# Reordering VectorE's token step in the front of a fused tokenizer, attention and FP4 feed-forward kernel, with one subtraction moved from GpSimd

## The reference

```python
# tokenizer
y = layernorm(patches, ln1_g, ln1_b) @ Wp + bp
h = concatenate([layernorm(y, ln2_g, ln2_b), txt], axis=1)
# differential attention, 8 heads, each the difference of two softmax maps
q, k, v = x @ Wq.T, x @ Wk.T, x @ Wv.T            # x = layernorm(h)
q, k = rotary(rmsnorm(q)), rotary(rmsnorm(k))     # 16 heads of 16
attn = softmax(q1 k1) - lam * softmax(q2 k2)      # causal
h = h + (layernorm(attn @ v) * (1 - LAMBDA_INIT)) @ Wproj.T
# feed-forward, weights and activations rounded to FP4 in blocks of 16
scale = max(|block|) / 6;  fp4(x) = grid[searchsorted(mid, |x / scale|)] * sign(x) * scale
h = h + fp4(silu(fp4(x) @ fp4(w_gate).T) * (fp4(x) @ fp4(w_up).T)) @ fp4(w_down).T
```

## Time and profile before

| what | value |
|---|---|
| median of 3 runs | 659.81 us (658.97 to 660.0) |
| the profiled execution's own time | 662.52 us |
| its span in the trace | 660.8 us |
| mean granted TensorE clock | 0.948 |
| busy share PE / DVE / ACT / POOL | 87% / 84% / 49% / 47% |

### The profile page before, as it was taken

The page is one execution under the profiler, slowest core; times in us unless marked ns, Lnnn a source line. Parts: engine busy times, 40 slices in busy tenths (PEclk is TensorE's granted clock), DMA queues, the critical chain, the costliest instruction groups (busy, mean ns, idle before and its releaser), DMA issues. The chain is left out here.

```text
span 660.8 us, 14226 instructions
## 1 busy us (share of the span) xinstructions
PE 576.4 (87%) x3666; PEld 470.0 (71%) x3666; DVE 554.1 (84%) x1444; ACT 322.1 (49%) x760; POOL 309.8 (47%) x455
## 2 busy tenths in 40 slices
PE   5665568999999999999999998589999999999996
PEld 4554455767776776777677676478888888888885
DVE  5999847898889889888988985498888888888884
ACT  2242215655665665566565564244544444445442
POOL 2455523555455445545554553155455445545542
PEclk9878776999999999999999997789999999999999
DMA  6900000011111111111111101111111111111111
GB/s 173 325 17 23 24 16 18 27 38 41 30 40 35 35 35 38 40 34 37 35 41 29 42 23 46 30 39 49 48 54 52 54 48 54 49 48 48 57 32 35
DMA packets 33734, 31.99 MB, mean 48 GB/s; under 512 B 6098, under 2 KB 32050, under 8 KB 33714
## 3 DMA queue, kind: packets, MB, share of 16 engines
q1 hardware_dynamic: 33714, 31.75, 16.3%
HBM read 23.02 MB, written 8.71 MB: 48 GB/s over the span
## 5 line engine op out<-in xcount | busy, mean ns | idle before, releaser
L741 PE MATMUL bank<-v_sb,pt 113*113 113x33 f32 x1024 | 109.1, 262 | 0.0
L741 PEld LDWEIGHTS bank<-v_sb,pt 113*113 113x113 f32 x1024 | 108.4, 181 | 0.7 <-issue 0.7
L858 POOL TENSOR_SCALAR_AFFINE_SELECT pt<-pt 113x452 f32<-113x452 f32 x128 | 73.9, 600 | 68.5 <-ACT pt L798 68.5
L798 ACT ACTIVATE pt<-bank 113x452 f32<-113x452 f32 x128 | 63.1, 545 | 38.2 <-PE bank L729 38.2
L138 PE MATMUL bank<-wgu_hi,fx_hi 128*128 128x512 f32 x174 | 69.5, 399 | 8.0 <-DVE fx_lo L1131 8.0
L1177 POOL TENSOR_TENSOR h_deq<-fh,fhb 128x704 f32<-128x704 f32 x29 | 40.3, 1389 | 68.8 <-DVE fhb L1084 56.3
L729 PE MATMUL bank<-q_blk,k_t 64*113 64x452 f32 x256 | 67.7, 605 | 0.0
L138 PE MATMUL bank<-wgu_hi,fx_lo 128*128 128x512 f32 x174 | 66.8, 384 | 0.0
L138 PE MATMUL bank<-wgu_lo,fx_hi 128*128 128x512 f32 x174 | 66.7, 384 | 0.0
L138 PE MATMUL bank<-wqkv_hi,xo_hi 128*113 128x256 f32 (+1 forms) x128 | 50.3, 393 | 17.7 <-DVE xo_lo L923 17.7
L1191 POOL TENSOR_TENSOR fh<-fh,fhb 128x704 f32<-128x704 f32 x29 | 40.3, 1391 | 42.2 <-DVE fhb L1145 42.2
(11 more groups left out here) (160 smaller groups left out, 1531.3 us busy)
## 6 DMA issues: line engine op xcount, KB each, us to landing
xb<-h_dram SPq DMA_DIRECT2D x29, 129.0 KB, 2.1
rb<-h_dram SPq DMA_DIRECT2D x29, 128.0 KB, 2.0
h_dram<-h SPq DMA_DIRECT2D x32, 112.9 KB
out<-res SPq DMA_DIRECT2D x28, 128.0 KB, 1.7
px<-in_patches SPq DMA_DIRECT2D x9, 384.0 KB, 10.1
hx<-in_txt SPq DMA_DIRECT2D x32, 77.0 KB
hr<-in_txt SPq DMA_DIRECT2D x32, 77.0 KB
wf<-in_wgu SPq DMA_DIRECT2D x1, 1408.0 KB, 8.0
```

The source lines that it names most:

```text
L741: mm = pe.matmul(pv_ps[s % 2][0:T, s // 2, :], pt[0:T, s, :], v_sb[0:T, s // 2, :], start=True, stop=True, skip_group_check=True)
L798: act.activation(pt[0:T, GS * g:GS * (g + 1), :].rearrange("p s t -> p (s t)"), sc_ps[g % 2][0:T, :], ACT.Exp, scale=1.0 / math.sqrt(HD)). ...
L858: pool.affine_select(out=grp, in_=grp, compare_op=ALU.is_ge, fill=0.0, base=0, pattern=[[0, GS], [1, T]], channel_multiplier=-1).then_inc( ...
```

## The change

In VectorE's list the statistics of the next patch tile come first in a step, ahead of the Newton step, and in step 0 ahead of the centring of the weights too; `w_low` and `token_sums` come before `w_round` and `w_codes`; the means of the value weights come before the maxima. On ScalarE `w_high` comes before `w_magnitude`. `attn_low` is issued by VectorE at the end of steps 4 and 5, and no more by GpSimd. No instruction is added or removed in all.

```diff
+            def attn_low(c):
+                dve.wait_ge(k["attn_high"], 2)
+                dve.tensor_tensor(wqkv_lo[:, c, :], wqkv_raw[:, c, :], wqkv_hi[:, c, :].bitcast(F32),
+                                  ALU.subtract).then_inc(k["attn_low"], 1)
+                dve.tensor_tensor(wproj_lo[:, c, :], wproj_raw[:, c, :], wproj_hi[:, c, :].bitcast(F32),
+                                  ALU.subtract).then_inc(k["attn_low"], 1)
...
             def steps(i):                                  # VectorE
+                slot(i, ((1, patch_sums, PT),))
+                if i == 0:
+                    centre_weights()
                 if roots_exist(i - 1):
                     newton_step(i)
-                if i == 0:
-                    centre_weights()
-                slot(i, ((-1, token_apply, PT), (1, patch_sums, PT), (0, w_round, NP), (0, w_codes, NP),
-                         (-1, w_low, NP), (0, token_sums, PT)))
+                slot(i, ((-1, token_apply, PT), (-1, w_low, NP), (0, token_sums, PT)))
                 if roots_exist(i):
                     variances(i)
+                slot(i, ((0, w_round, NP), (0, w_codes, NP)))
                 if i == -1:
                     gain_weights()
-                slot(i, ((1, w_maxima, NP), (-QKV_STEP, v_means, 1),
+                slot(i, ((-QKV_STEP, v_means, 1), (1, w_maxima, NP), (-QKV_STEP - 2, attn_low, KD),
                          (-LAMBDA_STEP, lambda_dots, 1), (-LAMBDA_STEP - 1, lambda_sum, 1)))
...
             def steps(i):                                  # ScalarE
-                slot(i, ((0, w_magnitude, NP), (-1, w_high, NP), (1, patch_copy, PT)))
+                slot(i, ((-1, w_high, NP), (0, w_magnitude, NP), (1, patch_copy, PT)))
...
             def steps(i):                                  # GpSimd
                 slot(i, ((-1, gain, PT), (0, w_dequantise, NP), (1, w_quotients, NP),
-                         (-QKV_STEP, v_subtract, 1), (-QKV_STEP - 2, attn_low, KD)))
+                         (-QKV_STEP, v_subtract, 1)))
```

## The result

| | kernel before | changed kernel |
|---|---|---|
| median of 4 and 4 runs, first group | 659.39 us | 667.90 us (665.13 to 670.61) |
| ratio with 95% interval | | 1.0131 [1.0086, 1.0176] |
| profiled execution, its span | 662.52, 660.8 us | 665.13, 663.4 us |
| ratio in two later groups, two chips, 9 runs each | | 1.0074 [1.0051, 1.0097] and 1.0078 [1.005, 1.0105] |

The forecast was 662.5 us with a range of 658.8 to 664.9. The direction holds, the size does not: +8.5 us by the first four runs, +4.9 and +5.1 us by the later ones (the ratio times 659.9 and 660.4), where +2.75 was forecast. In the later groups the runs of either kernel differ among each other by 4.5 to 7.2 us, and the profiled execution of the changed kernel was the shortest of its four.

A forecast was written before the change was run, and what follows sets the result against it. VectorE sets the pace of the front's middle steps; after the change it waits on a ring through TensorE. Step 0's 2.2 us plus 0.55 for the rings made +2.75 us, 662.5 us, range 658.8 to 664.9.

The forecast's parts named there:

- The Newton step: VectorE's front steps: with patch statistics covering GpSimd's quotient, it is late by some 0.25 us instead of 0.75.
- the subtractions: `attn_low` on VectorE, steps 4 and 5: 0.95 + 0.35 us and a 1.06 us wait for the quotient, 2.35 in all.
- Step 0: Front's first step: rounding no longer runs under the first projection, so the reciprocal ends at 25.25 instead of 23.05, losing 2.2 us.
- the step with the value means: Ring for piece 3: VectorE sets it at the high clock, value means stalled by dequantise some 0.85 us; 8.3 us.
- The ring through TensorE: L450 to L450 through dequantise, transposes, projection and L408: 7.37 us at high clock, 8.81 at low; more with two transpose groups.
- so I take the middle, 52.05, or +0.55: Step 0's reciprocal to the last: 49.8 us at high clock, 54.3 at low, 51.5 before; middle clock's chance 0.40.
- piece 2: Front ring with a dequantise of 704 columns, 0.33 us more: 7.7 us at the high clock or 9.1 at the low.
- piece 3: Front ring: 8.3 us at the high clock, where VectorE sets it, or 9.7 at the low.
- piece 4: Front ring with two groups of transposes: 8.0 us at the high clock or 9.7 at the low.
- every new step: TensorE idles 3.1 us from the end of the patch transposes to the next weight transposes.
- The rival with the low clock in every ring: Front rings all at TensorE's low clock: 2.2 + 2.8 = +5.0, 664.8 us; chance 0.18.
- The rest shifts along: Behind step 6: piece 7's L444 and L450 come 0.85 us late, but VectorE idles there anyway, so no further loss.

The follow-up runs named there:

- b3: Changed kernel with TensorE's weight transposes of a piece moved behind the next tile's projection: 1.0026 of the kernel before, +1.7 us.
- d3: Changed kernel with weight transposes behind the next projection and, in step 0 alone, the rounding ahead of the token sums: 1.0001 of the kernel before, +0.1 us.
- b2: Changed kernel with the rounding back ahead of the readers of PSUM in every step: 1.0006 of the kernel before, +0.4 us.
- c2: Changed kernel with three more matmuls, results unread, ahead of each projection of steps 2 to 6: 1.012 of the kernel before, +7.9 us.
- c1: Kernel before with three more matmuls, results unread, ahead of each projection of steps 2 to 6: 1.0004 of the kernel before, +0.3 us.
- a2: Changed kernel with the two subtractions of the attention weights back on GpSimd: 1.0067 of the kernel before, +4.4 us.
- a3: Kernel before, its order kept, with only the two subtractions of the attention weights moved to VectorE: 0.9999 of the kernel before, -0.1 us.
- a1: Changed kernel timed again with no edit: 1.0074 of the kernel before, +4.9 us.
- d1: Changed kernel timed a third time with no edit: 1.0078 of the kernel before, +5.1 us.

## Why the prediction was wrong in size

**VectorE's own terms held, but for one.** The Newton step is 0.21 to 0.25 us late by the quotient (L382 0.37), forecast 0.25; L433 takes 0.37 longer than its 0.18, forecast 0.4; L450 is down to 0.69; the subtractions take 0.89 and 1.27 with the quotient stretched to 1.64. Step 0: 2.2 us forecast, 2.2 in all three profiles of the changed kernel. With the ring open (b3, d3) the changed order takes 49.4 us from the reciprocal of step 0 to the last one, forecast 49.8. Only the step with the value means takes 8.96 us there, forecast 8.3.

**The ring through TensorE is real.** It was forecast as what VectorE waits for. Opened from VectorE's side (b2) the loss is 0.4 us, from TensorE's side 1.7 (b3), with step 0 mended too 0.1 (d3); lengthened (c2) it grows where the order of before takes the same for nothing (c1). From the reciprocal of step 0 to the last one the three profiles of the changed kernel take 52.2, 54.9 and 53.6 us, 2.7 to 5.4 more than the 49.4 with the ring open. The moved subtractions have no part in it (a2, a3).

**The step that failed is "so I take the middle, 52.05, or +0.55".** From L408 of step 0 to the last reciprocal the three profiles of the changed kernel take 57.23, 59.91 and 58.69 us, 58.6 in the mean, against 54.32 before: +4.3. Less step 0 that is +2.1 for the rings, with single runs at +0.7, +3.4 and +2.2. Ring by ring, from one end of L450 to the next:

| ring | forecast high, low, middle | three profiles |
|---|---|---|
| piece 2 | 7.7, 9.1, 8.4 | 8.93, 9.22, 9.66 |
| piece 3 | 8.3, 9.7, 9.0 | 9.37, 9.37, 8.96 |
| piece 4 | 8.0, 9.7, 8.85 | 7.68, 10.42, 9.16 |

The largest error is the ring of piece 2, 0.9 us above the middle in the mean. The forecast gave it the idle time of "every new step", 3.1 us; TensorE idled 7.63 us there, and its projection took 3.70, 3.99 and 4.43 us, never the 2.83 of the high-clock price. The low-clock projection was also priced too low, by the one row of 3.96 us, over which the granted clock is 0.69; a1's 4.67 has 0.59, so that its ring of piece 4 was 10.4 us, not 9.7, and wholly at the low clock it is 5.46 (d3). And the middle was taken between the levels by counting projections of the kernel before, where they came behind other idle times.

The rival with the low clock in every ring gave +5.0, and the later timings are +4.9 and +5.1; that they meet is luck in part, as the rings themselves brought 2.1 of its 2.8 us. The Trainium skill ("TensorE: Matmul & The Clock Gate", section "HAM oscillation — how this bites in real kernels"), cited for that rival, says that a kernel whose bursts are divided by long enough waits falls back to the low clock at each of them. The traces agree in part, since one or two projections of steps 2 to 6 in each of the three profiles of the changed kernel ran at 2.75 to 2.76 us.

**"The rest shifts along" is neither shown nor refuted.** From the last reciprocal to the second L408 behind 80 us the three profiles of the changed kernel take 24.2, 22.7 and 24.2 us, the two of before 24.2 and 21.9. The means differ by 0.6, the profiles of the one kernel by 2.4. In full the profiled spans are 5.7 us apart in the mean (664.4 and 658.7): 4.3 from L408 of step 0 to the last reciprocal, 0.6 here, and 0.4 each ahead of the one L408 and behind the other; the last three are within what one kernel varies by. The one profile used for the forecast had the two projections behind 80 us at 4.42 and 4.14 us, the second profile of before has them at 2.83 and 3.34.

**Open.** The first group's four runs gave +8.5 us, and neither later group of nine repeats it. The mean granted clock of these four is 0.944 to 0.951, that of the eighteen later ones 0.946 to 0.956. The profile of d1 is of an execution of 667.80 us, as long as that group's median, and shows nothing new. Against the first profile of before its span is 5.3 us longer: 4.4 from L408 of step 0 to the last reciprocal and 0.9 ahead of it, none behind. Whether such executions were frequent there by chance or by something in that group isn't settled. Nor is what decides, step by step, at which clock a projection runs. The intervals of the three ratios overlap just: 1.0086 against 1.0097 and 1.0105.

## What to carry to other kernels

Before moving an instruction on the busiest engine, follow what its result feeds on the other engines until it comes back: here the rounding fed the dequantise, the transposes and, by queue order alone, the next projection, so that moving it behind 2.5 us of other work in its step closed a loop whose links had all been hidden. Price an exposed TensorE link at the low clock, by a projection that ran wholly at it (5.46 us here, 2.75 at the high one), look at the idle time ahead of each one by itself, and use several profiles where an engine's clock enters the path. Lay two edits of different kind apart: the statistics first gave 0.2 to 0.5%, and the reordering that came with them cost more.

## What the runs showed of the hardware

- A VectorE instruction with two SBUF inputs and a GpSimd one keep each other out both ways. GpSimd's quotient took 1.64 us beside VectorE's subtraction of 0.89, and 1.06 beside patch statistics (d1); L474 took 1.27 us and ended 0.28 after that quotient.
- More TensorE work made the kernel faster: with 6 unread matmuls a step it went from +4.9 to +1.1 us, on the same chip, and the mean granted clock of a run rose from between 0.946 and 0.956 to between 0.956 and 0.969.
- The same 12 matmul records of a projection lasted from 2.75 us (granted clock 1.00) to 5.46 us (0.50). Where VectorE led, in the kernel before, the stretch from L408 of step 0 to the last reciprocal repeated within 0.01 us in two profiles; where it waited for TensorE, it varied by 2.7 us (57.23 to 59.91).
- Idle times of TensorE of the same length, 3.34 us, were followed by projections of 2.75 to 4.67 us in one and the same kernel.
